# A four-layer graph network on one core: the second layer's sigmoid, residual sum and statistics taken tile by tile into its gather loop

## What is computed

```python
h = jnp.maximum(_layernorm(x, axis=-1), 0.0)
x = x + _L1_gnn_ref(h, adj, adj, ...)

def _L1_gnn_ref(x, adj_a, adj_b, W_sa, a_sa, W_gcnb, b_gcnb, Wa, ba, Wb, bb):
    type_sum_a = adj_a @ x
    type_sum_b = adj_b @ x
    attn_a = jax.nn.sigmoid(jnp.concatenate([type_sum_a, x], axis=1) @ Wa.T + ba)
    attn_b = jax.nn.sigmoid(jnp.concatenate([type_sum_b, x], axis=1) @ Wb.T + bb)
    h = x @ W_sa
    s_left = h @ a_sa[0, :Hd]
    s_right = h @ a_sa[0, Hd:]
    scores = s_left[:, None] + s_right[None, :]
    e = jnp.where(adj_a != 0, jnp.exp(-jax.nn.leaky_relu(scores, 0.01)), 0.0)
    attn = e / (jnp.sum(e, axis=1, keepdims=True) + 1e-05)
    x_a = attn @ h
    x_b = adj_b @ (x @ W_gcnb) + b_gcnb
    return jax.nn.sigmoid(attn_a * x_a + attn_b * x_b)
```

## Time and profile before

| | us |
|---|---|
| median of 3 runs | 1142.24 |
| lowest and highest | 1139.75 and 1144.46 |
| the profiled execution | 1141.84 |
| its span (first to last instruction) | 1140.0 |

### The profile page before, as it was taken

One profiled execution on the slowest core, in us unless ns is written; L12 is line 12 of the kernel. 1 busy time (PEld: TensorE's weight loads), 2 busy tenths in 40 slices (PEclk: granted clock), 3 DMA queues, 4 the chain that ended last, 5 costly groups with the idle time before them and its releaser, 6 DMA issues. The chain is left out here.

```text
span 1140.0 us, 13951 instructions
## 1 busy us (share of the span) xinstructions
PE 932.0 (82%) x4807; PEld 769.5 (67%) x4807; DVE 751.3 (66%) x1284; ACT 523.4 (46%) x898; POOL 39.0 (3%) x101
## 2 busy tenths in 40 slices
PE   4998799959999799996879777997779389851885
PEld 3787688849899798995658636886534135641774
DVE  4653455454566545775479995323579999998996
ACT  4104655345332343223768824424478892225333
POOL 0000000000100001000140000000100000000000
PEclk9998899979999899998889988998889789995998
DMA  9000000000000000001205400000301110000001
GB/s 353 23 1 1 22 1 1 1 1 1 1 0 0 19 1 1 1 0 47 53 2 151 128 0 1 0 19 1 88 23 54 50 27 25 0 1 1 1 0 49
DMA packets 42896, 32.68 MB, mean 29 GB/s; under 512 B 3218, under 2 KB 40796, under 8 KB 42844
## 3 DMA queue, kind: packets, MB, share of 16 engines
q1 hardware_dynamic: 42844, 32.02, 9.2%
HBM read 30.63 MB, written 1.39 MB: 28 GB/s over the span
## 5 line engine op out<-in xcount | busy, mean ns | idle before, releaser
L604 ACT ACTIVATE u_rows_a<-e_rows,small 128x1354 f32<-128x1354 f32 x104 | 146.7, 1413 | 19.4 <-DVE small L1363 19.4
L795 PE MATMUL out<-feat,adj_t 128*128 128x256 f32 (+1 forms) x484 | 107.5, 380 | 1.5 <-DVE x_rows L1139 1.5
L824 PE MATMUL out<-h_rows,adj_strip 128*128 128x256 f32 x484 | 108.6, 381 | 0.0
L795 PEld LDWEIGHTS out<-feat,adj_t 128*128 128x128 f32 x484 | 91.4, 189 | 15.6 <-DVE x_rows L1139 1.9
L824 PEld LDWEIGHTS out<-h_rows,adj_strip 128*128 128x128 f32 x484 | 91.2, 192 | 11.7
L939 PE MATMUL scores<-feat_fb,adj_strip 128*128 128x512 f32 x154 | 73.4, 635 | 16.5 <-ACT feat_fb L629 13.0
L1369 DVE SCALAR_TENSOR_TENSOR tmp<-e_rows,small 128x1354 f32<-128x1354 f32 x52 | 84.5, 1625 | 0.0
L724 PE MATMUL turned_ps<-ident,tmp 128*128 128x128 f32 x132 | 30.9, 333 | 53.4 <-ACT tmp L436 36.2
L939 PEld LDWEIGHTS scores<-feat_fb,adj_strip 128*128 128x128 f32 x154 | 31.3, 206 | 55.9 <-issue 38.7
L1369 DVE SCALAR_TENSOR_TENSOR kept_tile<-e_rows,small 128x1354 f32<-128x1354 f32 x39 | 63.4, 1626 | 0.0
L724 PEld LDWEIGHTS turned_ps<-ident,tmp 128*128 128x128 f32 x132 | 18.5, 167 | 60.8 <-issue 32.2
(11 more groups left out here) (346 smaller groups left out, 2120.1 us busy)
## 6 DMA issues: line engine op xcount, KB each, us to landing
adj_strip<-in_adjT SPq DMA_DIRECT2D x22, 704.0 KB, 4.6
adj_t<-in_adjT SPq DMA_DIRECT2D x11, 704.0 KB, 12.9
u_weights<-in_L_gnn_U SPq DMA_DIRECT2D x8, 256.0 KB, 4.9
x_rows<-in_x SPq DMA_DIRECT2D x2, 512.0 KB, 3.9
tmp<-in_L_gnn_W_stack SPq DMA_DIRECT2D x2, 512.0 KB, 4.5
out_rows<-y_rows SPq DMA_DIRECT2D x2, 512.0 KB
tmp<-in_L_gnn_U SPq DMA_DIRECT2D x2, 256.0 KB, 2.9
x_rows<-in_x SPq DMA_DIRECT2D x1, 384.0 KB, 6.2
```

The costliest lines, as they stand in the source:

```text
L604: act.activation(out2[:, (k % 2) * N:(k % 2 + 1) * N], E[:, t, :], [ACT.Relu, ACT.Sign][k % 2], bias=nudged[:, t:t + 1], accum_out=[relu_s ...
L795: ins = pe.matmul(bank[:, 0:n], AT[:, j, cols(t)], features[:, j, 0:n], start=(j == 0), stop=(j == NT - 1))
L824: ins = pe.matmul(OUT[b][:, 0:D], ADJ[:, b, j, :], H[:, j, :], start=(j == 0), stop=(j == NT - 1))
```

## The change

- The left half of the score is projected for two tiles at once, at odd places of the ring, with 256 columns in one of two banks (`left_bank`), and copied by ACT in one piece of two tiles (`left_part`); the last tile goes alone.
- PE runs the plain gather one tile ahead, and its results alternate between OUT[0] and a bank of the scores (`l1b_bank`). The semaphore values GAL1A and GAL1B follow the new order.
- The sigmoid becomes 1 / (1 + exp(-u)): ACT takes the exponential of each tile of 256 columns two turns behind (`sig_l1`), DVE adds 1 and takes the reciprocal, adds the tile to x, and takes its statistics and their aggregate (`add_l1`), each step waiting for the one before it.
- DVE reads b(t) before a(t-1), and the third layer's weight split stands between the sums of tiles 8 and 9.
- The row sums and memsets stand between the variance and the use of the root.

```diff
-GAL1A = [GA["L1b"] + 2 * t + 2 for t in range(NT)]
-GAL1B = [GA["L1b"] + 2 * t + 1 for t in range(NT)]
+GAL1A = [GA["L1b"] + min(2 * t + 3, 2 * NT) for t in range(NT)]
+GAL1B = [GA["L1b"] + max(2 * t, 1) for t in range(NT)]
...
+        l1b_bank = [OUT[0], SC[:, 0:BANK]]
...
+        def left_bank(r):
+
+            return pbank[r // 2][2]
...
+            def left_part(t, r):
+                c, n = turned_width(t, r)
+                return act.activation(SLB[:, bass.ds(c, n)], left_bank(r)[:, 0:n], ACT.Copy) if n else None
...
-                copy_part(lambda t: SLB[:, cols(t)], 2, 0, P))
+                left_part)
...
+            def sig_l1(t):
+
+                act.wait_ge(gather_read, GAL1A[t])
+                act.activation(U1B[:, t, :], U1B[:, t, :], ACT.Exp, scale=-1.0).then_inc(sig_out, 1)
 
             z_l1(0)
             for t in range(NT):
...
                     gate_l1(t - 1)
+                if t >= 2:
+                    sig_l1(t - 2)
             gate_l1(NT - 1)
+            sig_l1(NT - 2)
             split_w("L2a", WH[:, :, 0:2 * D], raw[:, :, 0:2 * D])
-
-            for t0, t1 in PIECES:
-                act.wait_ge(gather_read, GAL1A[t1 - 1])
-                act.activation(U1B[:, t0:t1, :], U1B[:, t0:t1, :], ACT.Sigmoid).then_inc(sig_out, 1)
+            sig_l1(NT - 1)
...
             def gather_l1b(t):
-                if t >= 1:
-                    pe.wait_ge(gather_read, GAL1B[t - 1])
-                gather_adj(OUT[0], F1, t, D + 3)
+                if t >= 2:
+                    pe.wait_ge(gather_read, GAL1B[t - 2])
+                gather_adj(l1b_bank[t % 2], F1, t, D + 3)
...
             def proj_l1(t, r):
+                blocks_read(PJ["L1"], t, r)
+                _, n = turned_width(t, r)
+                if n:
+                    rows_times_turned(r + 1 - n // P, r + 1, left_bank(r)[:, 0:n], WrH, WrL, 0)
                 rows_read(PJ["L1"], t)
                 bank = pbank[r % 2]
                 rows_times(r, bank[0][:, 0:D + 6], WH, WL, 0, D + 6)
-                rows_times(r, bank[1][:, 0:D], WH, WL, D + 6, D)
-                return rows_times_turned(r, r + 1, bank[2][:, 0:P], WrH, WrL, 0)
+                return rows_times(r, bank[1][:, 0:D], WH, WL, D + 6, D)
...
+            gather_l1b(0)
             for t in range(NT):
-                gather_l1b(t)
+                if t + 1 < NT:
+                    gather_l1b(t + 1)
                 gather_l1a(t)
...
-            def add_piece(k):
-
-                t0, t1 = PIECES[k]
-                dve.wait_ge(sig_out, k + 1)
-                then(dve.tensor_tensor(X[:, t0:t1, :], X[:, t0:t1, :], U1B[:, t0:t1, :], ALU.add))
-                for t in range(t0, t1):
-                    stat(t, X)
+            link_s = chain(l1_sum, 4)
+
+            def add_l1(t):
+
+                dve.wait_ge(sig_out, t + 1)
+                link_s(t, 1, dve.tensor_scalar(U1B[:, t, :], U1B[:, t, :], 1.0, None, ALU.add))
+                link_s(t, 2, dve.reciprocal(U1B[:, t, :], U1B[:, t, :]))
+                link_s(t, 3, dve.tensor_tensor(X[:, t, :], X[:, t, :], U1B[:, t, :], ALU.add))
+                link_s(t, 4, stat_of(t))
+                return dve.bn_aggr(mv[:, t, :], stats[:, t, :])
...
                 mask_l1(t)
+                read_l1b(t)
                 if t >= 1:
                     read_l1a(t - 1)
-                read_l1b(t)
+                if t >= 2:
+                    add_l1(t - 2)
             dve.wait_ge(ld_w, LD["L2a"])
             mark(raw_ready)
             split_w("L2a", WL[:, :, 0:2 * D], raw[:, :, 0:2 * D], WH[:, :, 0:2 * D])
+            add_l1(NT - 2)
             read_l1a(NT - 1)
-            add_piece(0)
-            add_piece(1)
-            add_piece(2)
+            then(add_l1(NT - 1))
+            dve.tensor_scalar(var[:, :], mv[:, :, 1], LN_EPS, None, ALU.add).then_inc(var_ready, 1)
...
-            norm_stats("L2")
...
             mark(x_l1)
+            norm_close("L2")
```

More of the change, by code:

```diff
@@ L242, in build @@
         limit_ready, row_diff, tie_mark = sem("limit_ready"), sem("row_diff"), sem("tie_mark")
-        end_step = sem("end_step")
+        end_step, l1_sum = sem("end_step"), sem("l1_sum")
         pads = sem("pads")
@@ L1206, in read_l1b @@
                 dve.wait_ge(gathered, GAL1B[t])
-                dve.tensor_tensor(tab[:, t, :], OUT[0][:, D:D + 2], vab[:, t, 0:2], ALU.add).then_inc(gate_in, 1)
-                dve.tensor_copy(rowsum[:, t:t + 1], OUT[0][:, D + 2:D + 3])
-                dve.tensor_tensor(U1B[:, t, :], OUT[0][:, 0:D], bgc[:, :], ALU.add).then_inc(gather_read, 1)
+                plain = l1b_bank[t % 2]
+                dve.tensor_tensor(tab[:, t, :], plain[:, D:D + 2], vab[:, t, 0:2], ALU.add).then_inc(gate_in, 1)
+                dve.tensor_copy(rowsum[:, t:t + 1], plain[:, D + 2:D + 3])
+                dve.tensor_tensor(U1B[:, t, :], plain[:, 0:D], bgc[:, :], ALU.add).then_inc(gather_read, 1)
             link_t = chain(dve_tail, 5)
@@ L1223, in read_l1a, with stat_of @@
                                          in1=U1B[:, t, :], op0=ALU.mult, op1=ALU.add).then_inc(gather_read, 1)
-            def add_piece(k):
-                t0, t1 = PIECES[k]
-                dve.wait_ge(sig_out, k + 1)
-                then(dve.tensor_tensor(X[:, t0:t1, :], X[:, t0:t1, :], U1B[:, t0:t1, :], ALU.add))
-                for t in range(t0, t1):
-                    stat(t, X)
+            link_s = chain(l1_sum, 4)
[6 more added lines that the diff above has]
+                return dve.bn_aggr(mv[:, t, :], stats[:, t, :])
+            def stat_of(t):
+                return dve.bn_stats(stats[:, t, :], X[:, t, :])
             lrelu_l1(0)
```

## The result

| | before | after |
|---|---|---|
| median (lowest to highest), 20 runs each | 1141.99 (1137.77 to 1144.46) | 1138.01 (1135.60 to 1142.00) |
| the profiled execution and its span | 1141.84, 1140.0 | 1140.71, 1138.8 |

The medians lie 4.0 us apart. The ratio over all runs is 0.9975, with a 95% interval of 0.9964 to 0.9987; by it the change takes 2.9 us off (1.5 to 4.1), where 9.4 were forecast, and the text goes by these ratios throughout. 1138.01 lies 5.2 above the forecast and outside its range.

The account below looks back on a forecast made before the run. The prediction took PE to bound the gather loop, with DVE and ACT half idle. Terms of -3.3, -7.4 and +1.3 summed to -9.4 us from 1141.84, with the median's 0.4 giving 1132.8 us, range 1128.0 to 1137.0.

Parts of the forecast that it names:

- part 1: Projection ahead of the gather loop: left sums for two tiles at once take 3.3 us off PE.
- part 2: Start of the gather loop: plain gather one ahead saves 7.4 us, 4.4 of stall and 3.0 of half-clock gather.
- part 3: Inside the loop: added ACT and DVE work stays hidden under PE, DVE at 8.2 of 9.6 us per tile.
- part 4: End of the loop: DVE's late queue puts normalisation 12.3 us after the last gather is seen, 1.3 us longer than before.
- the clock falls anyway: Start of the loop: case behind the lower bound, where only the 4.4 us stall goes and the half clock stays.
- Eight rounds per element: Rival on DVE's 256-column reciprocal: 2.26 us, three sums at the end cost 1.3 more, 1134.1 us; chance 0.15.
- the cheap reciprocal: Rival on DVE's 256-column reciprocal: 0.33 us, the end gains 4.5 over the forecast, 1128.3 us; chance 0.08.
- the projection at nothing: Rival on the projection: the readers' round becomes the bound on even tiles, no gain there, 1136.1 us; chance 0.08.
- DVE as the bound: Rival in the loop: reciprocal of 3.90 us, DVE needs 10.2 us per tile, kernel slower at 1144.6 us; chance 0.04.
- a stall that stays: Rival at the loop's start: something else is late, 4 us or more of the 7.4 are left, near 1138; chance 0.09.
- the sum: Whole kernel: -3.3 - 7.4 + 1.3 = -9.4 us, set against the profiled execution's 1141.84 us.

Follow-up runs that it names:

- left pair: The kernel before with only the left sums projected for two tiles at once: median 1141.22 us, ratio 0.9995 (0.9981 to 1.0009).
- gather ahead: The kernel before with only the plain gather one tile ahead and DVE's reading order to match: median 1138.07 us, ratio 0.9977.
- end order: The changed kernel with tile 8's sum and the weight split moved ahead of the last reads at the loop's end: median 1134.37 us, ratio 0.9933.

## Why the prediction was wrong, point by point

| term | forecast | traces, on average |
|---|---|---|
| part 1, left sums | -3.3 | -2.9 |
| part 2, plain gather ahead | -7.4 | -4.8 |
| part 3, loop | 0 | 0 |
| last gather's wait | none | +1.8 |
| part 4, the end | +1.3 | -1.2 |
| branch behind the flag | none | +2.3 |
| start of the kernel | none | +1.1 |
| sum | -9.4 | -3.7 |

- **Part 1** was near. From the first normalisation to the first gather it takes 32.2 us on average without the pair (seven traces, 31.68 to 33.45) and 29.3 with it (eleven, 28.80 to 30.06). The median of the left pair alone shows only 0.6 of it. Beside the gather ahead the pair gives 4.2 (0.9940 for 0.9977, on two chips, some 3 us uncertain).
- **Part 2** was mis-sized, 4.8 for 7.4. "4.4 of the stall and 3.0 of a gather at half clock" describes the trace of before, and holds for the three traces of its kind (7.3 to 7.7). It is not what the stage does on average: in three of six traces with the stall a low stretch lies over the first gather instead, where it costs nothing, since the attention gather waits for its mask in any case (9.47 or 9.48 us from one to the other in both kinds). With the gather ahead the same stretch costs 1.7. The stated lower bound of 4.4 "(the clock falls anyway)" left out this case, in which 3.0 are saved.
- **Part 3**: the reciprocal is 1.753 us, forecast 1.84; the exponential 0.40 to 0.42, forecast 0.41. DVE is busy 71.31 of 93.00 us, under the 8.2 per tile forecast. Eight rounds per element (2.26) and the cheap reciprocal (0.33) are both out, and so are the rivals with the projection at nothing, DVE as the bound and a stall that stays. The estimate from the Trainium skill's page "VectorE: DVE Perf Modes", section "First, the fixed hardware budget", was 2.13 for this row; the measurement decides.
- **Part 4** had the right order of DVE's queue: split, tile 9, read and tile 10 behind the last gather. From the sight of a(9) to the normalisation it forecast 4.8 + 12.3 = 17.1; the rows have 16.39. But it took the last gather to follow at once. PE waited for a(9)'s bank, and DVE worked on in that time. From the end of the last gather, about 227.61 + 5.06 = 232.67 by end order's own start and sight (228.22 and 233.28), it is 9.8, not 12.3; the wait, with PE's restart, is 1.8. Both together are +0.6 (102.45 from the fourth gather to the normalisation before, 103.05 now). That this is only 0.7 from the +1.3 is in part luck: a missed wait and too long an end set each other off.
- **Behind the changed stage** the prediction had no term at all, and that step failed most: "the sum" assumed that code which isn't changed takes its old time. It doesn't, where a program's length or its set of functions changes: 2.3 us at a branch 800 us later and 1.1 at the start.

Forecast -9.4, terms found -3.7, measured -2.9 (-1.5 to -4.1), so the terms lie within the interval. Two other averages agree. From the second layer's first normalisation to the fourth gather the five traces with neither part take 52.1 us and the ten with both 45.1, 7.0 less, for the 7.7 of parts 1 and 2. And from the third layer's first normalisation to the end of the span the ten traces with the short idle row take 890.9 us (888.9 to 894.3) and the seven with the long one 893.3 (892.3 to 896.3): 2.4 more, about the branch's 2.3. The 6.6 between the two traces of the result were that, and 4.2 of scatter: the one of before lay 1.2 below its group and the changed one 3.0 above. A sum made against one trace could not tell such scatter from a term.

## What to carry to other kernels

- A change in the number of instructions on an engine can change what a later taken branch of that engine costs. Where a kernel has one on the critical path, look for an "issue" row behind it before and after, and count instructions ahead of it; 98 tiny ones in idle time took 2.3 us off that row here.
- A half-clock stretch seen once in a trace need not be a term that an edit returns: the same edit gave 7.3 to 7.7 us or 3.0 here, by where the stretch lay. Compare it over several kernels that share the stage.
- When work is deferred behind a gather, ask at the last tile which gathers adjoin and share a bank, and put what needs nothing new (tile 8's sum, the weight split) into the idle time ahead of the last reads: 3.1 us here.

## What the runs showed that was not expected

- A branch's place in DVE's instruction stream costs 1.21 to 1.23 or 3.46 to 3.74 us of idle time between the same two instructions (ten and seven traces); 30 instructions more, 800 us ahead of it, brought the long row and 128 more than before took it away.
- Whether a program holds a Sigmoid changes when a DMA at its start lands: the bias 6.0 to 7.5 us behind its issue with one and 7.9 to 8.8 without, the first normalisation 1.1 us earlier with one.
- DVE's reciprocal of 128x256 takes 1753 ns, against 225 for 128x11 and 155 to 164 for 128x1: (1753 - 225)/245 = 6.2 ns per element, a slope that ten columns already showed.
- Filling PE's idle time with matmuls that nobody reads gained nothing that can be measured (1.0 us, from 2.6 less to 0.7 more); in its one trace the low clock lay over the gather ahead of the filled time.
